# A recommender tower in fixed-order chunks: two more groups spread by TensorE in chunk 0, layer 0's sums one chunk ahead instead of two, and the row split two groups later

## The reference, cut to what matters

```python
z0 = jnp.einsum('bid,bjd->bdij', x0, x0).reshape(B, D, F0 * F0)      # x0 = e, F0 = 39, D = 16
cur0 = jax.nn.relu(jnp.einsum('bdk,kl->bld', z0, W0))                # L = 128
next_h, direct0 = jnp.split(cur0, 2, axis=1)                         # 64 and 64
z1 = jnp.einsum('bid,bjd->bdij', x0, next_h).reshape(B, D, F0 * Fk)
cur1 = jax.nn.relu(jnp.einsum('bdk,kl->bld', z1, W1))
z = jnp.sum(jnp.concatenate([direct0, cur1], axis=1), axis=-1)
h = jnp.concatenate([z, dense_ctx], axis=1)                          # 208 columns
h = jnp.maximum(h @ W_top1 + b_top1, 0.0)                            # 512
h = jnp.maximum(h @ W_top2 + b_top2, 0.0)                            # 256
y = h @ W_top3
```

## Time and profile before

| | us |
|---|---|
| median of 3 runs (lowest, highest) | 422.27 (419.37, 424.58) |
| the profiled execution | 422.4 |
| its span, first to last instruction | 420.6 |
| PE busy | 394.9 (94%) |
| DVE busy | 346.2 (82%) |
| ACT busy | 227.3 (54%) |
| POOL busy | 267.3 (64%) |

### The profile page before, as it was taken

The page is one execution under the profiler, slowest core; times in us unless marked ns, Lnnn a source line. Parts: engine busy times, 40 slices in busy tenths (PEclk is TensorE's granted clock), DMA queues, the critical chain, the costliest instruction groups (busy, mean ns, idle before and its releaser), DMA issues.

```text
span 420.6 us, 4083 instructions
## 1 busy us (share of the span) xinstructions
PE 394.9 (94%) x1426; PEld 247.2 (59%) x1426; DVE 346.2 (82%) x198; ACT 227.3 (54%) x228; POOL 267.3 (64%) x164
## 2 busy tenths in 40 slices
PE   0896869999999999999999999999999999999997
PEld 0643526656565656565666666565656565666655
DVE  0115747989999999999999999998999989999930
ACT  1334445474756647484756574847557384745422
POOL 5775878988888888888888888888885000000000
PEclk9999979999999999999999999999999999999999
DMA  7194979389796969596979798896959495998000
GB/s 286 31 212 101 246 169 260 77 221 215 223 231 166 275 173 273 163 255 147 243 169 269 180 247 211 205 225 193 254 161 269 142 269 164 272 261 226 4 0 0
DMA packets 27862, 80.80 MB, mean 192 GB/s; under 512 B 7265, under 2 KB 16225, under 8 KB 20034
## 3 DMA queue, kind: packets, MB, share of 16 engines
q1 hardware_dynamic: 22354, 78.43, 71.3%
q0 software_dynamic: 5120, 1.32, 3.0%
q10 hardware_dynamic: 368, 0.80, 0.5%
HBM read 76.58 MB, written 3.93 MB: 191 GB/s over the span
## 4 chain that ended last, share of the span: by engine, by line
PE 62%; DMA 16%; issue 7%; DVE 7%; POOL 4%; SPq 2%; ACT 1%; ACTq 0%
PE acc L557 12%; PE acc L583 10%; PE acc L584 10%; PE acc L591 9%; PE acc L602 8%; DMA x_wide<-x_rows 6%; PE sums L525 5%; POOL found L299 4%; DMA found<-in_table_dram,rows_sb 4%; DVE z L445 4%; DMA x_rows<-found 3%; DMA x_parts<-x_rows 3%; PE acc L598 2%; DVE z_lo L453 2%; SPq L225 2%
## 5 line engine op out<-in xcount | busy, mean ns | idle before, releaser
L299 POOL DMA_INDIRECT found<-in_table_dram,rows_sb x160 | 267.1, 1670 | 53.9 <-issue 46.6
L351 ACT ACTIVATE z_hi<-z 128x2048 fp32r<-128x2048 f32 x63 | 120.4, 1911 | 69.2 <-DVE z L445 69.1
L453 DVE TENSOR_TENSOR z_lo<-z,z_hi 128x2048 fp32r<-128x2048 f32 x64 | 146.3, 2287 | 12.1 <-ACT z_hi L351 12.1
L445 DVE TENSOR_TENSOR z<-x_wide,h 128x2048 f32<-128x2048 f32 x64 | 145.4, 2286 | 2.2 <-DMA x_wide<-x_rows 2.2
L583 PE MATMUL acc<-z_hi,w_hi 128*128 128x512 f32 x256 | 107.3, 419 | 3.3 <-ACT z_hi L384 3.3
L557 PE MATMUL acc<-squares,w 128*128 128x512 f32 (+1 forms) x210 | 102.3, 604 | 4.2 <-ACT squares L318 4.2
L584 PE MATMUL acc<-z_hi,w_lo 128*128 128x512 f32 x256 | 100.2, 392 | 0.0
L591 PE MATMUL acc<-z_lo,w_hi 128*128 128x512 f32 x256 | 82.0, 442 | 1.3 <-DVE z_lo L453 1.3
L318 ACT ACTIVATE squares<-sums 128x1024 f32<-128x1024 f32 (+1 forms) x60 | 54.9, 915 | 41.9 <-issue 21.4
L591 PEld LDWEIGHTS acc<-z_lo,w_hi 128*128 128x128 f32 x256 | 48.0, 188 | 24.7 <-issue 14.9
L583 PEld LDWEIGHTS acc<-z_hi,w_hi 128*128 128x128 f32 x256 | 48.1, 188 | 18.4 <-issue 8.2
(11 more groups left out here) (60 smaller groups left out, 160.7 us busy)
## 6 DMA issues: line engine op xcount, KB each, us to landing
x_wide<-x_rows SPq DMA_DIRECT2D x64, 512.0 KB, 8.2
x_wide<-x_rows SPq DMA_DIRECT2D x112, 256.0 KB, 9.5
x_parts<-x_rows SPq DMA_DIRECT2D x31, 128.0 KB, 2.6
x_rows<-found SPq DMA_DIRECT2D x16, 240.0 KB, 2.4
x_wide<-x_rows SPq DMA_DIRECT2D x16, 192.0 KB, 6.9
found<-in_table_dram,rows_sb POOLq DMA_INDIRECT x160, 7.6
w_sb<-in_w_dram SPq DMA_DIRECT2D x1, 1280.0 KB, 8.5
x_wide<-x_rows SPq DMA_DIRECT2D x16, 64.0 KB, 6.5
```

What stands on the lines that cost most here:

```text
L299: pool.indirect_dma_start(out=found[:, b, 2, s * D:s * D + D], out_offset=None, in_=table, in_offset=bass.IndirectOffsetOnAxis(ap=rows_sb[ ...
L351: nc.scalar.activation(z_hi[:, n % RING], z[:, n % RING], ACT.Copy).then_inc(hi_done, 1)
L445: nc.vector.tensor_tensor(z[:, n % RING], x, h[:, c % 2, :].unsqueeze(1).to_broadcast([P, QUADS, N]), ALU.mult).then_inc(multiplied, 1)
L453: nc.vector.tensor_tensor(z_lo[:, n % RING], z[:, n % RING], z_hi[:, n % RING], ALU.subtract).then_inc(lo_done, 1)
```

## The change

Four things change; the arithmetic does not.

- In chunk 0, groups 3 and 4 are spread by PE too. `spread_once` does four 32-row matmuls with a third set of 0/1 matrices, `once_sb`, which is loaded by SP and copied by ACT. So broadcasts (0,2) and (0,3) of slots 2 and 3 fall away, and the broadcast for (0,2) moves behind chunk 1's lay-out. Which fields the slots hold is dealt anew.
- For chunks 2 to 7 all of layer 0's sums stand one chunk ahead (`LATE = 7`), in the order that chunk 2's had before.
- The splits of chunks 3 to 7 stand in step 3 instead of step 1. Chunk 2's stands later as well.
- The waits of `in_step` are looser for chunk 2 and one group earlier for chunk 3.

```diff
-WIDE_FROM = [[2, 6], [30, 33], [10, 18], [22, 26]]
+WIDE_FROM = [[2, 26], [30, 33], [10, 18], [6, 22]]
+SPREAD_ONCE = {3: ((0, 0), (0, 2), (0, 1), (0, 3)), 4: ((1, 1), (2, 1), (1, 0), (1, 2))}
+ONCE = 3
+LATE = 7
@@ sync
+            sp.dma_start(once_in, select_once).then_inc(once_in_done, 16)
             bring(0)
             widen(0, 0)
+            lay_out(1)
             widen(0, 1)
-            bring(1)
-            widen(0, 2)
-            widen(0, 3)
+            place(sp, 1, 0)
+            place(sp, 1, 1)
             widen(1, 0)
             widen(1, 1)
             bring(2)
@@ gpsimd
-                       (2, 0): (squared, 5), (2, 1): (squared, 6), (2, 2): (squared, T0), (2, 3): (h_ready, 2),
-                       (2, 5): (multiplied, 1), (2, 7): (lo_done, 1), (2, 9): (multiplied, 2),
-                       (3, 0): (multiplied, 2), (3, 3): (multiplied, 3), (3, 6): (multiplied, 4),
-                       (3, 9): (multiplied, G)}
+                       (2, 0): (squared, 4), (2, 1): (squared, 5), (2, 2): (squared, 6), (2, 3): (squared, T0),
+                       (2, 5): (h_ready, 1), (2, 7): (half_multiplied, 1), (3, 0): (multiplied, 1),
+                       (3, 3): (multiplied, 2), (3, 6): (multiplied, 3), (3, 9): (multiplied, 4)}
@@ scalar
+            act.wait_ge(once_in_done, 16)
+            nc.scalar.activation(once_sb[:, :, :].rearrange("p t m -> p (t m)"), once_in, ACT.Copy).then_inc(once_ready, 1)
...
-                    if g == 0 and c < 2:
+                    if g == 0 and c < LATE:
                         square(ND * (c + 1))
...
-                    if n == 0:
-                        split(2)
-                    if g > 2 and 0 < c < CHUNKS - 2:
+                    if g > 2 and LATE - 2 < c < CHUNKS - 2:
                         square(ND * (c + 2) + g - 3)
                     if 0 < n < G * CHUNKS - 1 and is_v(n + 1):
                         high_part(n + 1)
+                    if n == 2:
+                        split(2)
                     if g == 2 and c + 1 < CHUNKS:
                         evict0(c + 1)
-                    if g == 1 and 0 < c < CHUNKS - 2:
+                    if g == (3 if c < LATE - 1 else 1) and 0 < c < CHUNKS - 2:
                         split(c + 2)
@@ vector
+            dve.wait_ge(squared, 5)
             dve.wait_ge(w1_hi_ready, 1)
...
+                    if n == G - 2:
+                        split(2)
                     if is_v(n):
                         low_part(n)
                     if g == 1 and c:
                         reduce1(c - 1)
                     if n == 2:
                         reduce0(0)
-                        split(2)
-                    if g == 1 and 0 < c < CHUNKS - 2:
+                    if g == (3 if c < LATE - 1 else 1) and 0 < c < CHUNKS - 2:
                         split(c + 2)
@@ tensor
+            def spread_once(n, before):
+                if n == list(SPREAD_ONCE)[0]:
+                    pe.wait_ge(once_ready, 1)
+                pe.wait_ge(multiplied, before + 1)
+                for a, (m, q) in enumerate(SPREAD_ONCE[n]):
+                    rows = slice(32 * q, 32 * q + 32)
+                    last = nc.tensor.matmul(spread[:, a, :], once_sb[rows, m, :], x_parts[rows, 0, :],
+                                            start=True, stop=True)
+                last.then_inc(spread_done, 1)
...
             contract1_lo(0)
+            spread_once(3, 0)
             add_up(ND + 1)
...
             add_up(ND + 3)
+            spread_once(4, 3)
             contract0(ND + 2)
...
-                    if n == G:
-                        add_up(2 * ND)
+                    if g == 0 and c < LATE:
+                        add_up((c + 1) * ND)
                     if g == 0:
                         contract1_lo(n - 1)
-                    if n == G:
-                        add_up(2 * ND + 1)
-                        contract0(2 * ND)
+                    if g == 0 and c < LATE:
+                        add_up((c + 1) * ND + 1)
+                        contract0((c + 1) * ND)
...
-                    if g > 2 and c + 2 < CHUNKS:
+                    if g > 2 and LATE < c + 2 < CHUNKS:
                         add_up(ND * (c + 2) + g - 3)
-                    if g == G - 1 and c + 2 < CHUNKS:
+                    if g == G - 1 and LATE < c + 2 < CHUNKS:
                         contract0(ND * (c + 2))
```

More of the change, by code:

```diff
@@ L86, in pairs, with build @@
     return [order[P * t:P * t + P] for t in range(T0)]
-def build(nc, ids, table, select, w0a, w0b, mix, w1, wt1, bt1, wt2, bt2, wt3, dense, out):
+def build(nc, ids, table, select, select_once, w0a, w0b, mix, w1, wt1, bt1, wt2, bt2, wt3, dense, out):
     with ExitStack() as ctx:
@@ L109, in build @@
         select_sb = sb("select_sb", [P, T0 + len(SPREAD), P], F32R)
+        once_sb = sb("once_sb", [P, ONCE, P], F32R)
         w0 = sb("w0", [P, T0, P])
@@ L122, in build @@
         w0b_sb = staging[:, (T0 + len(SPREAD)) * P:(2 * T0 + len(SPREAD)) * P]
+        once_in = staging[:, (2 * T0 + len(SPREAD)) * P:(2 * T0 + len(SPREAD) + ONCE) * P]
         h = sb("h", [P, 2, N])
@@ L153, in build @@
         select_in_done = sem("select_in_done")
+        once_in_done = sem("once_in_done")
+        once_ready = sem("once_ready")
         w0_in = sem("w0_in")
@@ L196, in uses, with spreads @@
             return c // BUFS + 1
+        def spreads(c):
+            return len(SPREAD) * (c + 1) + len(SPREAD_ONCE)
         def place(queue, c, half):
@@ L244, in bring @@
                 if c >= BUFS:
-                    sp.wait_ge(spread_done, len(SPREAD) * (c - BUFS + 1))
+                    sp.wait_ge(spread_done, spreads(c - BUFS))
                     sp.wait_ge(summed, T0 * (c - BUFS + 1))
@@ L434, in multiply @@
                     dve.wait_ge(h_ready, 2 * (c + 1))
-                if g in SPREAD:
-                    dve.wait_ge(spread_done, len(SPREAD) * c + SPREAD.index(g) + 1)
+                if c == 0 and g in SPREAD_ONCE:
+                    dve.wait_ge(spread_done, len(SPREAD) + list(SPREAD_ONCE).index(g) + 1)
+                    x = spread[:, :, :]
+                elif g in SPREAD:
+                    dve.wait_ge(spread_done, spreads(c - 1) + SPREAD.index(g) + 1)
                     x = spread[:, :, :]
                 else:
-                    dve.wait_ge(wide_in[WIDE.index(g)], 16 * (4 if g == WHOLE else 3) * (c + 1))
+                    dve.wait_ge(wide_in[WIDE.index(g)],
+                                16 * (4 if g == WHOLE else 3) * (c + (g not in SPREAD_ONCE)))
                     x = x_wide[:, WIDE.index(g), :].rearrange("p (t n) -> p t n", n=N)
@@ L565, in spread_out @@
                     pe.wait_ge(multiplied, G * c + SPREAD[i - 1] + 1)
+                elif c == 1:
+                    pe.wait_ge(multiplied, list(SPREAD_ONCE)[-1] + 1)
                 elif c:
@@ L770, in layout @@
                 w1[HALF * a:HALF * a + HALF, slot1(g) + q] = from_w1[f]
+    select_once = np.zeros((P, ONCE, P), np.float32)
     for i, g in enumerate(WIDE):
@@ L778, in layout @@
                 w1[p, slot1(g) + k] = from_w1[f, p % HALF]
+                if g in SPREAD_ONCE:
+                    m, q = SPREAD_ONCE[g][k]
+                    row = [r for r in rows_of(f) if r // 32 == q][0]
+                    select_once[row:row + 2, m, p] = 1.0
     def by_tile(a):
@@ L786, in layout @@
         "select": select.reshape(P, (T0 + len(SPREAD)) * P),
+        "select_once": select_once.reshape(P, ONCE * P),
         "w0a": by_tile(w0a),
```

## The result

The changed kernel takes 447.32 us (median of 4; 444.87 to 453.43), the kernel before, run beside it, 423.42. The ratio is 1.0605, 95% interval 1.0536 to 1.0674: slower by 6%. I had said 442 us, 431 to 452. The profiled execution took 444.87 us. A ratio leaves out executions over 1.5% above the fastest of their kernel (three of e5's six), so it isn't always the quotient of the medians beside it.

The account below looks back on a forecast made before the run. It took a waiting start to about 66 us, then a loop set by PE. Start, four loops of 28.7 us and the way out gave 20.0 us later: span 440.6, plus 1.8, 442.4; predicted 442, range 431 to 452.

Parts of the forecast that it names:

- Part 3: Late split in group 3: lay-out, broadcasts, last multiply and split close a loop of 28.7 us a chunk against 22.26.
- Part 1: New start in chunks 0 and 1: multiply (chunk 1, group 0) at 57.4 instead of 66.07, 8.7 us gained.
- The first turn into the loop: Chunk 1's multiplies to chunk 3's lay-out: lay-out at 79.0 instead of about 81.5, using 6.2 of the gain.
- Part 2: Layer 0's sums one chunk ahead in chunks 2 to 7: cost taken as 0, bounds 0 and 1.3 us.
- The way out of the loops: Chunk 7's lay-out at 193.8, chunk 8's at 214.5, its x_parts 5.5 us later at 220.0 instead of sums at 200.00.
- Rival A: TensorE's clock falls in each late chunk, 3.4 us lost a chunk, 17 us more in all: 459 us; chance 0.07.
- Rival B: Late broadcasts land within 17.3 us of the lay-out and are hidden, only the start counts: 413.7 us; chance 0.08.
- Rival C: Lateness doesn't add up over chunks; chunk 2's first broadcast there at 90.4, end gains 4 us: 418; chance 0.08.
- What I asked to see: Lay-outs 28.7 us apart, DVE idle some 5 us a chunk, PE under 85% busy, 22.3 again from chunk 7.

Follow-up runs that it names:

- e5: Changed kernel with LATE = 2, so only the new start is left and later sums and splits stand as before: 416.91 us, 0.982 of the kernel before.
- e1: Changed kernel with the splits of chunks 3 to 7 back in group 1, all else as changed: 428.15 us, 1.0196 of the kernel before.
- e3: Changed kernel with LATE = 4, so only chunks 3 and 4 are split late: 429.96 us, 1.0189 of the kernel before.
- e9: Changed kernel with the splits of chunks 3 to 7 in group 2, one step earlier: 425.36 us, 1.0149 of the kernel before.
- e2: Changed kernel with SP issuing three of four broadcasts before the next lay-out and x_parts in chunks 1 to 5: 435.60 us, 1.0355 of the kernel before.
- e11: Kernel with only the new start, plus eight unused matmuls on PE before chunk 1's first sums: 418.02 us, 0.9948 of the kernel before.
- e12: Kernel with only the new start (LATE = 2), measured once more: 418.25 us, 0.9925 of the kernel before.
- e10: Kernel with only the new start, but with the kernel before's waits for chunk 2's and 3's gathers: 419.71 us, 0.998 of the kernel before.
- e6: Kernel before with only layer 0's sums of chunks 3 to 7 moved one chunk ahead; old start, splits in group 1: 424.2 us, 1.0051.
- e4: Changed kernel with 12 unused matmuls on PE before the first sums of chunks 3 to 7: 450.62 us, 1.0651 of the kernel before.
- e7: e5 with reduce0 on DVE moved one step later, from chunk 2 on: 439.01 us, 1.0416 of the kernel before.
- e8: Kernel before with only reduce0 on DVE moved one step later: 442.24 us, 1.0483 of the kernel before.

## Why the prediction was right, step by step

- **Part 3, the loop: right.** Worked out 28.7 us a chunk, measured 28.7 to 29.2. e1 takes the cause away, e3 shows that it acts per chunk, e9 that it follows the split's place (23.1 expected, 23.3 measured). The terms hold one by one: 23.3, 23.7, 23.4, 22.9 and 22.1 us from lay-out to the last broadcast for chunks 3 to 7, 23.7 taken. The four loops came out 0.7 us longer.
- **Part 1, the start: right in this execution, and less sure than I wrote.** (0,4) at 50.21 (51.3 said), (1,0) at 56.45 (57.4 said). Of the eleven profiles with this start five have (1,0) at 56.3 to 56.5, e2's at 58.5, and five at 61.3 to 63.6, as e11 and e12. I had `x_parts` of chunk 1 at 40 to 41; in e5 it is there at 38.9, in e11 and e12 at 43 to 44. Chunk 1's lay-out goes with it: 33.2 to 34.5 in those five, 30.8 to 31.1 in the other six. Behind it stands the gather that waits for DVE's copy of `w` (`w0_ready`): it starts at 21.39 in e5 and at 22.79 in e12, 23.38 in e10. What makes that copy late I have not separated.
- **The first turn into the loop: 1.2 us too low.** Chunk 3's lay-out came at 80.23, 79.0 said. (1,4) started at 73.61, 0.4 earlier than said, but its 5.0 us to the lay-out were 6.6: ACT evicted h of chunk 2, three operations of 0.6 us, before it rounded (1,4), and DVE's split waited 1.71 us. In chunks 2 to 5 this way took 5.9, 5.0, 5.4 and 5.9 us.
- **Part 2, nothing: too low in itself**, by 2 us with the old start (e6) and by 11 with the new (e1 against e5). That it did no harm to the sum was in part luck: here the loop is longer than a chunk of POOL's gathers, and hides them. The reason that I gave was another, that PE is not the bound.
- **The way out of the loops: 0.8 us too low.** From chunk 7's lay-out to 8's it was 19.3 us, 20.7 said. From chunk 8's lay-out to its sums it was 7.7 us, 5.5 said: the lay-out itself landed after 3.5 us, among chunk 6's broadcasts, which then were still running. I had taken 2.3 us from the earlier trace rows; the same trace has lay-outs of 3.3 to 3.9 us too, for chunks 9 and 12 to 14, which I had not looked at.
- **In all:** 20.0 us said, 22.8 at chunk 8's sums (1.2, 0.7 and 0.8 more) and 22.5 in the spans. The median lies 5 us above my 442: 2.5 are this sum, and the rest is that the profiled execution was the fastest of four.
- **Rival A** is right that the clock falls in each late chunk, down to 0.88 over a stretch, and wrong on its price, 17 us: e4. The rule of the Trainium skill (TensorE: Matmul & The Clock Gate, "HAM oscillation") describes what the trace shows, a clock that falls in each round of a loop that waits for a DMA. Whether the fall costs time hangs on whether the engine is the bound; here it was not.
- **Rival B** falls: behind a later lay-out the last broadcast landed after 22.1 to 23.7 us, no faster than before. **Rival C** falls by e3. (Its 11.4 us to the first broadcast didn't fit the sum's own 10.9; (2,1) started 10.9 us behind the lay-out.)
- **What I asked to see:** PE under 85% busy came out at 83 to 87%; the rest is there nearly as written, with the idle ahead of the multiplies at 6.4 us a chunk rather than 5, and with two more gaps of 24.3 and 22.9 us behind chunk 8 before it is 22.3 again.
- **What I did not see at all:** the gathers. They are the next bound once the late split is gone, and take 2.5 of the 9.3 us that the good start gains. My prediction of the changed kernel was safe from them because the late split leaves them time: chunk 5's had landed at 112.8 us, and its split came at 137.7. So it was in e2, where five are held 9.6 us and from 66 us on the splits wait 2.3 us for gathers in all. For e1, e7 and e8 the same omission gave misses of 10 to 22 us.

What stays open: why a gather gets in at the next change of operation in one case and passes up to four in another (below), and whether the 9 us hold in chunk 1 goes when chunk 1's own `reduce0` is moved away from the low part behind it; that was not tried.

## What to carry to other kernels

When a step is moved behind others on its engine, follow what its result releases on other queues and back to that engine: if the way closes and is longer than the old period, its length is the new one, and it can be added up from rows. A queue issued in program order carries lateness to everything behind it. Idle time that appears after such a change, and a clock that falls with it, were its signs here and not its cause; fill the idle time once and see whether the period moves. Where a small operation stands can matter more than how long it takes: look at what other engines start right behind it. And keep the part of a change that pays: the new start alone runs at 416.91 and 418.25 us, 0.982 and 0.9925 of the kernel before.

## What the runs showed of the hardware

**A gather on POOL can be held by DVE for 5 to 10 us, and which one is held hangs on fractions of a microsecond.** While DVE is idle a gather takes 0.94 us. Beside DVE's unbroken row it normally takes 1.90; POOL, then DVE, of the kernel before:

```profile
97.94 1.90 POOL L299 DMA_INDIRECT found<-in_table_dram,rows_sb  x1 [0.30 <-issue]
100.14 1.90 POOL L299 DMA_INDIRECT found<-in_table_dram,rows_sb  x1 [0.30 <-issue]
...
111.98 0.94 POOL L299 DMA_INDIRECT found<-in_table_dram,rows_sb  x1 [0.30 <-issue]
```

```profile
96.73 2.28 DVE L453 TENSOR_TENSOR z_lo<-z,z_hi 128x2048 fp32r<-128x2048 f32 x1
98.93 2.29 DVE L445 TENSOR_TENSOR z<-x_wide,h 128x2048 f32<-128x2048 f32 x1
...
111.37 2.27 DVE L445 TENSOR_TENSOR z<-spread,h 128x2048 f32<-128x2048 f32 x1
```

The gather of 97.94 ends at 99.84, 0.91 us after DVE's change of operation at 98.93; the next is issued 1.21 us into that operation and gets in at the next change. The gather of 111.98 isn't held at all: DVE's operation reads `spread`, which is in PSUM and not in SBUF. Counted over the 14 profiles (2240 gathers):

- 206 were issued up to 1.7 us into a 128x2048 multiply from `spread`. All took 0.94 or 0.95 us.
- 806 were issued 1.0 us or more into a multiply from `x_wide` or a low part, which read both inputs from SBUF. None took more than 2.1 us.
- 427 were issued earlier than that into one. 46 of them took 4.5 to 9.7 us, the others 3.1 at most.
- Of those issued 0.55 to 0.61 us in, 35 of 41 were held over 4 us in a low part and none of 34 in a multiply from `x_wide`.

Nearly all of the held ones ended 0.8 to 0.9 us after DVE fell idle or began a `reduce`. Five in e1 and e6 (7.8 to 10.0 us) were issued 1.85 us into a multiply from `spread`, 0.35 us before a low part.

This fits e7 and e8. A gather that gets in when a `reduce` starts sets the next one 1.21 us behind that start, and the `reduce` lasts 0.60 us to the next operation: 0.61 us. In the kernel before, the operation behind `reduce0` is the multiply from `spread`, and all ten gathers issued 0.60 to 0.62 us into it took 0.94 or 0.95 us. In e8 it is a low part, and all twelve issued 0.60 or 0.61 us into it took 4.7 to 6.9. The 9.14 us of e5 is of this kind too, behind chunk 1's `reduce0`. That is read from positions in the traces; why a low part holds such a gather over further operations isn't settled.

The Trainium skill, SBUF — State Buffer, section "Who interferes with whom", says that a DVE instruction with two inputs in SBUF contends with a GpSimd instruction that reads SBUF. The 1.90 us beside such operations and the 0.94 beside one that reads PSUM agree. The section also tells of a probe in which `tensor_tensor` did not stall a DMA; here it does. The 4.5 to 10.0 us, over up to four changes of instruction, go beyond it.
